# Strided attention: the second quarter of the context is loaded before the first routed layer's last scatters and projected directly behind the first quarter

## What is computed

```python
x = x + tanh(g_xattn[0]) * L0_xattn(ctx_1024, layernorm(x), ...)      # perceiver attention
x = x + tanh(g_ffn[0])   * L0_ffn(layernorm(x), ...)                  # first routed layer, 4 experts, top 2
x = x + tanh(g_xattn[1]) * L1_xattn(layernorm(x), ctx_1024, ..., 16)  # strided attention
x = x + tanh(g_ffn[1])   * L1_ffn(layernorm(x), ...)                  # second routed layer, 8 experts, top 2

# L1_xattn, 16 heads of 32, stride 16: head h sees context rows h, h + 16, h + 32, ... (45 of them)
Q = (hidden @ Wq.T + bq);  K = (ctx @ Wk.T + bk);  V = (ctx @ Wv.T + bv)      # split into heads
Kg, Vg = K[:, h, idx_h], V[:, h, idx_h]                                        # idx_h = h + 16 * arange(45)
out = softmax(Q @ Kg.T * 32 ** -0.5) @ Vg
return out @ Wo.T + bo
```

## Time and profile before

| | us |
|---|---|
| median of 3 runs (lowest, highest) | 2107.54 (2104.54, 2107.74) |
| the profiled execution, its own time | 2116.41 |
| its span | 2114.7 |
| TensorE busy in the span | 1932.6 (91%) |
| mean granted TensorE clock | 0.959 of full speed |

### The profile page before, as it was taken

One profiled execution on the slowest core, in us unless ns is written; L12 is line 12 of the kernel. 1 busy time (PEld: TensorE's weight loads), 2 busy tenths in 40 slices (PEclk: granted clock), 3 DMA queues, 4 the chain that ended last, 5 costly groups with the idle time before them and its releaser, 6 DMA issues. The chain is left out here.

```text
span 2114.7 us, 35637 instructions
## 1 busy us (share of the span) xinstructions
PE 1932.6 (91%) x12328; PEld 1570.0 (74%) x12328; DVE 1022.1 (48%) x2243; ACT 842.6 (40%) x1792; POOL 659.5 (31%) x555
## 2 busy tenths in 40 slices
PE   5889999999999999999859999999997885999983
PEld 3568878787777778787648888888884665999983
DVE  6324555555555545544464323333335656554544
ACT  3223443433434443434434323333323534655540
POOL 4011020303030111200034445555422104787872
PEclk9899999999999999999969999999998986999997
DMA  7630101010011102000053213333349125545546
GB/s 207 205 122 1 54 14 52 19 52 19 30 33 35 37 9 59 12 17 17 5 177 120 94 66 113 111 105 109 119 154 314 33 87 168 167 172 167 191 140 205
DMA packets 111912, 201.58 MB, mean 95 GB/s; under 512 B 31520, under 2 KB 32320, under 8 KB 111252
## 3 DMA queue, kind: packets, MB, share of 16 engines
q1 hardware_dynamic: 106964, 183.93, 26.5%
q0 software_dynamic: 4800, 15.73, 2.2%
HBM read 171.64 MB, written 27.98 MB: 94 GB/s over the span
## 5 line engine op out<-in xcount | busy, mean ns | idle before, releaser
L461 POOL TENSOR_TENSOR a_rows<-a_rows,a_gain_x 128x512 f32<-128x512 f32 (+1 forms) x48 | 68.3, 1422 | 555.8 <-DVE a_rows L876 555.8
L620 PE MATMUL a_kv_ps<-a_kvin_hi,a_wk_hi 128*128 128x512 f32 (+1 forms) x512 | 196.2, 383 | 1.0 <-DVE a_kvin_lo L883 1.0
L1094 PE MATMUL f_banks<-f_wab_hi,f_x_hi 128*128 x448 | 185.4, 414 | 1.3 <-DVE f_x_lo L1766 1.3
L621 PE MATMUL a_kv_ps<-a_kvin_lo,a_wk_hi 128*128 128x512 f32 (+1 forms) x512 | 180.4, 352 | 0.0
L622 PE MATMUL a_kv_ps<-a_kvin_hi,a_wk_lo 128*128 128x512 f32 (+1 forms) x512 | 180.3, 352 | 0.0
L1096 PE MATMUL f_banks<-f_wab_hi,f_x_lo 128*128 x448 | 177.1, 395 | 0.0
L1095 PE MATMUL f_banks<-f_wab_lo,f_x_hi 128*128 x448 | 175.8, 392 | 0.0
L543 ACT ACTIVATE a_probs<-a_probs,a_neg_max 100x822 f32<-100x822 f32 x128 | 125.9, 984 | 113.1 <-DVE a_neg_max L907 112.9
L1788 DVE TENSOR_TENSOR f_h_sb<-f_h_sb,f_banks 128x256 f32<-128x256 f32 x112 | 47.2, 422 | 244.4 <-ACT f_h_sb L1511 243.4
L1511 ACT ACTIVATE f_h_sb<-f_banks 128x256 f32<-128x256 f32 x112 | 43.0, 384 | 294.1 <-PE f_banks L1096 294.1
L1094 PE MATMUL m_banks<-m_wab_hi,m_x_hi 128*128 x512 | 155.8, 304 | 2.5 <-DVE m_x_lo L1766 1.7
(11 more groups left out here) (411 smaller groups left out, 4876.0 us busy)
## 6 DMA issues: line engine op xcount, KB each, us to landing
f_raw<-f_pieces SPq DMA_DIRECT2D x94, 256.0 KB, 2.7
m_raw<-m_pieces SPq DMA_DIRECT2D x92, 256.0 KB, 2.8
f_wab_raw<-f_pieces SPq DMA_DIRECT2D x42, 512.0 KB, 6.3
m_wab_raw<-m_pieces SPq DMA_DIRECT2D x42, 512.0 KB, 6.4
a_rows<-ctx SPq DMA_DIRECT2D x8, 1280.0 KB
ahead_piece<-g_ctx SPq DMA_DIRECT2D x2, 2880.0 KB, 19.2
a_wout_sb<-L_xattn_Wkv SPq DMA_DIRECT2D x8, 512.0 KB, 15.4
m_y_acc<-m_pieces SPq DMA_DIRECT2D x8, 512.0 KB, 6.2
```

Of the source, the lines that this page charges most:

```text
L461: own.link(nc.gpsimd.tensor_tensor(row, row, gain_x[0:n, :], ALU.mult))
L620: nc.tensor.matmul(out, hi_l, hi_r, start=first, stop=False)
L621: nc.tensor.matmul(out, hi_l, lo_r, start=False, stop=False)
L1094: nc.tensor.matmul(out, left_hi, right_hi, start=start, stop=False)
```

## The change

The load of piece 1 moves from behind the sums of batches 0 to 3 to the end of the routed layer, directly behind the loads of `x_mid`, in both branches there. TensorE projects piece 1 directly behind piece 0, ahead of the transposes; ScalarE copies its keys and values between the first two square roots; the token copies of all four batches follow; the turns of the PSUM banks follow the new order. No instruction is added or removed.

```diff
@@ gated_experts, sync, branch with more than CORE slots
                     ahead.load_piece(sp, 0)
                     handed.load_stream(sp)
+                    ahead.load_piece(sp, 1)
@@ strided_attention
-        for kind, n in (("k", 0), ("v", 0), *(("x", b) for b in range(HB)), ("k", 1), ("v", 1), *(("q", m) for m in range(KD)),
+        for kind, n in (("k", 0), ("v", 0), ("k", 1), ("v", 1), *(("x", b) for b in range(HB)), *(("q", m) for m in range(KD)),
@@ sync
             sums.load_half(sp, 0)
-            ahead.load_piece(sp, 1)
             sp.dma_start(wq_raw[:, :, :], wq_t).then_inc(wq_loaded, 16)
@@ scalar
-            for g in range(2):
-                deviations(g)
-                for b in EQUAL[g]:
-                    move_tokens(b)
+            deviations(0)
+            move_keys(1)
+            move_values(1)
+            deviations(1)
+            for b in range(HB):
+                move_tokens(b)
             act.wait_ge(wq_loaded, 16)
             for k in range(KD):
                 nc.scalar.activation(wq_hi[:, k, :], wq_raw[:, k, :], ACT.Copy).then_inc(wq_hi_done, 1)
-            move_keys(1)
-            move_values(1)
@@ tensor
             context(0)
+            context(1)
             pe.wait_ge(const_done, 3)
             for b in range(HB):
                 tokens(b)
-            context(1)
             pe.wait_ge(wq_lo_done, KD)
             half(0)
```

## The result

The changed kernel takes 1.0020 times as long as the kernel before, with a 95% interval of 1.0013 to 1.0027 (medians 2111.3 and 2106.82 us of 20 runs each): 4.2 us slower, between 2.7 and 5.7. Forecast were 2.15 us slower, that is 2109.7 us, with 2104.0 to 2113.0 as the range.

What follows compares the result with a forecast made beforehand. The prediction took the stage's first half as bound by a chain of last scatter, sums, VectorE and queries. -4.15 + 4.2 (late sums) + 2.1 (clock) = +2.15 us gave 2109.7 us, range 2104.0 to 2113.0.

Steps and rivals of the forecast that it cites:

- The chain: First half of the attention stage: last scatter, sums landed, VectorE, queries, then third projection; change = -4.15 + d + c.
- -4.15: Third projection's start with nothing late: from 1633.76 to 1629.61 us, a gain of 4.15 us.
- d: Lateness of the first sums from loading piece 1 early; 4.0 to 4.6 us, taken as 4.2.
- c: Cost to the queries of starting at 1.2 GHz; 1.7 to 2.8 us, taken as 2.1.
- the forecast's own case: Piece 1 on q1 holds back ten scatters on q0 until about 1596.5; they end at 1602.7 to 1603.3; chance 0.48.
- a sign that it was wrong: In the profile after, scatters and piece 1 moving side by side would mean the forecast was wrong, the result better.
- The lower bound of d: 0.6 us, if the engines move all three streams, 7.1 MB, at 0.42 MB/us from 1582 on, to 1599.2.
- Rival 1: Fair sharing: scatters take turns beside piece 1 and end near 1599; d = 1.6, change -0.4 us, 2107.1 us; chance 0.22.
- The row from 1582 to 1589: Profile row during x_mid's load: q1 holds the DMA engines at 99.0%, q0 absent although four scatters were issued.
- Rival 3: GpSimd has room for four outstanding scatters only; d = 6.8 to 6.9, change +4.8 us, 2112.3 us; chance 0.14.
- the returns read from the earlier trace: TensorE's three returns to full clock, at about 1604.1, 1621.1 and 1669.0, after 5.5, 4.2 and 3.3 us at half rate.
- The cover: TensorE's idle time from 1606.39 takes the moved 4.97 us projection, ending at 1611.4 against first tokens at 1611.31.

Runs made afterwards that it cites:

- e1: Kernel before with piece 1 loaded early, as in the changed kernel, but all engines in their old order; ratio to the kernel before 1.0018 (1.0005 to 1.0030).
- e5: Kernel before with piece 1 in four transfers, two of them loaded early; ratio to the kernel before 1.0043 (1.0029 to 1.0058).
- e7: e4 with unused matmuls, seven behind the first projection and three after the second token batch; ratio to the kernel before 1.0007 (0.9994 to 1.0021).
- e10: Changed kernel with piece 1 issued ahead of the residual stream; single run without interval, sums issued 5.0 us after the first context matmul.
- e11: e9 with piece 1 ahead of the residual stream's first half; ratio to the kernel before 0.9999 (0.9987 to 1.0011).
- e4: Kernel before with piece 1 in four transfers, one of them loaded early; ratio to the kernel before 0.9986 (0.9972 to 0.9999).
- e2: Changed kernel with piece 1 loaded at its old place, the new TensorE and ScalarE order kept; ratio to the kernel before 1.0033 (1.0016 to 1.0051).
- e6: Kernel before with unused matmuls, seven behind the first projection and three after the second token batch; ratio to the kernel before 1.0001 (0.9992 to 1.0010).
- e3: Changed kernel with 18 unused matmuls in TensorE's waits; ratio to the kernel before 0.9997 (0.9986 to 1.0008).
- e8: Changed kernel with the residual stream's second half loaded behind the query weights; ratio to the kernel before 0.9998 (0.9985 to 1.0011).
- e9: e8 with unused matmuls (5, 3 and 5) in TensorE's waits; ratio to the kernel before 0.9994 (0.9983 to 1.0004).

## Why the prediction was right in direction and small by half

- **The chain held, the picture of the queues didn't.** The early load paid with the scatters' end, and with d and c read from the profile the sum -4.15 + d + c comes out right at the third projection in both profiles of the changed kernel: -4.15 + 6.4 + 1.3 = 3.5 us (measured 38.7 - 35.2 = 3.5), and -4.15 + 6.3 + 2.4 = 4.5 (39.7 - 35.2). So nothing else entered up to there. But scatters held back for the whole of piece 1, the forecast's own case, is not what happened. They moved side by side with it, which the prediction named as a sign that it was wrong and that the time would be better. The time was worse. In either picture all the bytes pass the same engines ahead of the sums; on that the direction rested, and that part was right.
- **d was the term mis-sized: taken 4.2, measured 6.4 (11.08 - 4.71).** I let q1 run first and the scatters behind it, at the engines' full 0.42 MB/us, to the end. In fact 5.6 MB took some 15.7 us from 1586 on, instead of the 13.2 us of my sum. Until about 1599.6 the queues moved 5.3 MB at 0.39 MB/us, 1.0 us longer than at 0.42; the last 0.3 MB took 2 us and not 0.7. A sum of bytes by peak rate has no tail in it. (The lower bound of d, 0.6, should by its own numbers be 0.3: 7.1 MB at 0.42 MB/us from 1582 on end at 1598.9.)
- **Rival 1 was right about the queues and wrong about its price.** q0 got its turns once x_mid was through, as the rule cited with that rival has it, but 0.14 MB/us is less than the 0.19 that GpSimd issues, so the scatters did not end near 1599 of before. The row from 1582 to 1589, on which I rested the forecast, was right for 5.8 us after the first scatter was handed over, and for less than 1 us of piece 1. The Trainium skill's rule of turns packet by packet ("DMA: Bandwidth & Descriptors", "Queues, rings and completion order") agrees with the 11 us after it, in which the queues moved 506 and 449 packets, and not with the 5.8 us before, in which five scatters were issued and none moved.
- **Rival 3 did not happen**: GpSimd issued the last scatter 2.3 us before t0 as before, with some six outstanding by then (ten handed over, 2.62 MB, and 1.04 MB moved from 1580 to 1593.8).
- **c was 1.3 and 2.4 us in two profiles, taken 2.1.** Of the returns read from the earlier trace rows, 1604.1 and 1621.1 lie 0.1 to 0.2 us too early, which hardly moves c. A second fall, in the second half's queries, cost about 1.6 us in the first profile and nothing in the second. I hadn't foreseen it. It makes the loss at the scores 3.5 + 1.6 = 5.1 us there, of which 4.2 show in the ratio. It came in six of the fourteen profiles (changed, e1, e5, e7, e10, e11) and not in the others, and what decides it is open.
- **The cover held**: both projections fit into the idle time, ScalarE's moved copies cost nothing (VectorE needs 12.36 us from its first combine to the low tokens in both profiles), and the waits for the query weights and for piece 2 went. What the runs leave open is why e4, e5 and the two measurements of the changed kernel differ from their marks by up to some 5 us.

## What to carry to other kernels

In this kernel a load moved ahead of a transfer on the critical path cost most of its own length at that transfer's end (1.4 of 1.8 us for a quarter, 6.3 to 6.6 of 7.0 for the whole), though it was on another queue and though the engines looked partly idle there. Look for the last transfer before the wait, add what stands in front of it by the time for which it fills the engines and not by its bytes, and add a tail. Idle time on TensorE that is "free" for an early matmul may be bought with exactly the transfers that end the idle time. And where TensorE waits in pieces, see what the work behind the wait pays for the fallen clock before filling the wait with something that needs new bytes.

## What the runs showed of the hardware

- After a burst is queued on q1, the scatters of q0 get nothing for some us and then a share. The first q0 packets come 4.6 to 4.9 us after the first of these scatters was handed over where only the residual stream is on q1 (before, e2, e6), 5.5 to 6.0 us where part or all of piece 1 follows it (both profiles of the changed kernel, e1, e3, e4, e5, e7), 4.3 to 4.4 us where half the stream stands before piece 1 (e8, e9), and 3.2 to 3.3 us where piece 1 is first (e10, e11). What ends the hold is open.
- Once both queues moved, they moved 506 and 449 packets in 11 us, of 5.4 and 3.4 KB: the queue with the smaller packets got the smaller share of the bytes (changed kernel).
- The order of two loads on one queue changed the end of a third transfer by 2.1 to 2.3 us at equal bytes (e10, one profile).
- Matmuls that compute nothing kept the granted clock at 2.4 GHz from the tokens to the second half's queries (e3; without them the waits are 7.17, 2.53 and 3.64 us long). They were worth 2.5 to 3.1 us at the first scores; the ratio became 0.9997, where the changed kernel had 1.0020 and 1.0010. With seven of them instead of ten behind a single projection the clock fell all the same (e6), with 3.64 us of idle time left before the first tokens.
